# Corners of gathered taps summed by identity products on TensorE, with corner weights in PSUM

## The chip, the cores and the metric

One NeuronCore of a Trainium2 chip runs the kernel. The metric is the device time of one execution in microseconds (us).

## The reference

A feature map x of 256 channels and 32 x 32 pixels, float32, goes through four blocks. Block 0 is a masked bottleneck of grouped convolutions with a residual. Blocks 1 and 2 are bottlenecks around a **deformable 3 x 3 convolution** of 64 channels: a small convolution gives for each pixel and each of nine taps a displacement, block 1 also a factor (a sigmoid), the 64 channels are sampled at the displaced place by bilinear interpolation, and the samples are contracted with the 3 x 3 weights. Block 1 has group norms, block 2 has biases. Block 3 is a non-local block (theta, phi, g) with a normalisation over pixels. Of the sampling, per tap:

```python
out = g(y0, x0) * (wy0 * wx0)[:, None, :] + g(y0, x0 + 1) * (wy0 * wx1)[:, None, :] + g(y0 + 1, x0) * (wy1 * wx0)[:, None, :] + g(y0 + 1, x0 + 1) * (wy1 * wx1)[:, None, :]
```

where g looks up 64 channels at an integer pixel, and gives zero outside the image.

## The kernel before

The program is written by hand, one instruction stream per engine, with semaphores between them. The blocks follow one another. All the change lies in the sampling of blocks 1 and 2, which the code calls b = 0 and b = 1 and this text the first and the second **sampling loop**.

The nine taps are computed in two ways at once. Three of them, the **dense** taps, need no gather: for each of 8 tiles of 128 source pixels ScalarE writes |y distance| into PSUM (L751, "near"), VectorE turns it into a hat function times the x hat (L558, "product", output S, one of four buffers which show in the profile as S, x and mask), and TensorE multiplies with the 64 channels (L937, "dense"): 3 x 8 = 24 **chunks** per loop, each of two matmuls, one for each half of the 1024 pixels. For each of these taps TensorE first spreads x position, y position and, in the first loop, the modulation over 128 partitions (L923, "positions": one matmul per half of the pixels), and ScalarE reads these two halves out (L709, L731, L721). The two halves go to two PSUM banks, `B_FILL = [1, 3]`, which later taps use again.

The other six taps are **gathered**. GpSimd issues 48 indirect DMAs per loop (L348: 8 tiles of 128 pixels x 6 taps), each of which fetches for 128 pixels all four corners x 64 channels into G. G holds five tiles. The work on them goes in 16 **units** u per loop, two for each tile: 4 taps (even u), then 2 taps (odd u). For one unit VectorE multiplies the four corners with their weights (L571, GW, weights from the SBUF tile corner_w), adds them pairwise (L579, GA) and once more (L586, GS). TensorE transposes GS, two taps at a time (L981: 2 transposes or 1), ScalarE copies the result to SBUF (L778, sT), and TensorE contracts it with the weights two units later (L951).

The order is written out. On VectorE unit u is GW, one product, GA, further products, GS. The table BESIDE says how many chunks stand beside each unit: `[0, 0, 2, 1, 3, 2, 2, 2, 2, 2, 2, 2, 2, 1, 1, 0]`. On TensorE unit u is its chunks, the contraction of unit u - 2, a wait for GS of u and for the copy sT of u - 1, the transposes, in units 0 and 1 some matmuls that keep the clock up (L823, 6 and 2 of them), and the positions of a later tap where one is due. In the last two units of the second loop there are two residual matmuls each (L835), and after unit 15 come two of `last_conv3` (L893). On ScalarE unit u is its near chunks, the copy sT, and the reading of positions.

## Time and profile before

| | |
|---|---|
| median of 3 runs | 242.93 us (242.92 to 243.75) |
| profiled execution: span from the first to the last instruction | 242.3 us |
| mean granted TensorE clock | 0.872 |
| PE, DVE, ACT, POOL busy | 191.5, 169.3, 110.8, 116.2 us |
| first loop: first gather to last gather issued | 37.4 to 107.4 us |
| second loop: first gather to last gather issued | 140.7 to 209.5 us |

Only the span is given for the profiled execution; the median of the runs lies 0.6 us above it. PE is TensorE's matmuls, PEld its weight loads, DVE VectorE, ACT ScalarE, POOL GpSimd, SP the queue that issues plain DMAs. Times on the axis are from the first instruction. A float32 matmul shows as two records in the trace, so that "x4" in a row of L937 is the two matmuls of one chunk; a transpose or an fp32r matmul shows as one. A row of several records gives the time from the start of the first to the end of the last, and each matmul's duration holds its way through the array besides the time for which it occupies it.

### The profile page before, as it was taken

How to read it: one execution, taken by the hardware profiler on the slowest of the kernel's cores; microseconds unless marked ns; L12 is line 12 of the kernel's file. 1: busy time of each engine (PE TensorE's matmuls, PEld its weight loads, DVE VectorE, ACT ScalarE, POOL GpSimd, SP SyncE). 2: the span in 40 equal slices, each digit the busy share in tenths (PEclk: the TensorE clock that was granted, in tenths of full speed). 3: DMA queues.
4: the chain of work that ended last, by engine and by line, in shares of the span. 5: the costliest groups of instructions: out<-in, count | busy, mean ns of one | idle time of the engine just before them, and what ended most of it. 6: DMA issues, size and time to landing. Idle time of an engine off the chain costs nothing. (4 is left out here: it accounts for less than half of the span.)

```text
span 242.3 us, 2580 instructions
## 1 busy us (share of the span) xinstructions
PE 191.5 (79%) x894; PEld 106.8 (44%) x894; DVE 169.3 (70%) x276; ACT 110.8 (46%) x163; POOL 116.2 (48%) x111
## 2 busy tenths in 40 slices
PE   8997998767678959749977989395796868799920
PEld 8362957553222423316763677352332323334500
DVE  1996624698999999964375343989999799522362
ACT  2122303567969866301106133769798562034022
POOL 5000006777787787750010067787788777400010
PEclk9999998559997997995999975589999979999855
DMA  6500022323322222230000223323322233300004
GB/s 228 225 0 3 0 87 65 105 72 98 97 88 88 89 65 87 87 108 1 3 0 0 87 62 99 102 80 98 104 68 66 87 97 99 87 3 0 0 0 173
DMA packets 7887, 17.60 MB, mean 73 GB/s; under 512 B 1729, under 2 KB 3906, under 8 KB 7746
## 3 DMA queue, kind: packets, MB, share of 16 engines
q0 software_dynamic: 4608, 12.59, 17.2%
q1 hardware_dynamic: 3122, 4.32, 5.1%
q10 hardware_dynamic: 144, 0.52, 0.5%
q8 instruction: 7, 0.11, 0.2%
q14 instruction: 6, 0.05, 0.1%
HBM read 15.33 MB, written 2.10 MB: 72 GB/s over the span
## 5 line engine op out<-in xcount | busy, mean ns | idle before, releaser
L348 POOL DMA_INDIRECT G<-table,idx x96 | 110.1, 1147 | 53.8 <-issue 43.2
L751 ACT ACTIVATE ps<-pos_y,second 128x1024 f32<-128x1024 f32 x48 | 52.9, 1115 | 17.6 <-DVE S L558 8.5
L981 PE MATMUL ps<-first,GS 128*128 128x128 f32 x48 | 13.3, 334 | 31.7 <-DVE GS L586 31.6
L571 DVE TENSOR_TENSOR GW<-G,corner_w 128x1024 f32<-128x1024 f32 (+1 forms) x32 | 30.6, 955 | 7.1 <-DMA G<-table,idx 6.9
L335 POOL TENSOR_TENSOR rstd<-var,half_neg 128x1 f32<-128x1 f32 (+1 forms) x4 | 2.6, 639 | 63.5 <-DVE var L398 39.7
L558 DVE SCALAR_TENSOR_TENSOR x<-ps,hat_x 128x1024 f32<-128x1024 f32 x24 | 29.1, 1213 | 0.0
L823 PE MATMUL ps<-first 128*128 128x128 f32 x180 | 28.2, 314 | 0.0
L823 PEld LDWEIGHTS ps<-first 128*128 128x128 f32 x180 | 25.8, 224 | 4.2 <-issue 3.9
L937 PE MATMUL ps<-x,V 128*64 128x512 f32 x96 | 27.1, 643 | 0.0
L981 PEld LDWEIGHTS ps<-first,GS 128*128 128x128 f32 x48 | 5.8, 149 | 39.8 <-DVE GS L586 38.3
L778 ACT ACTIVATE sT<-ps 128x256 f32<-128x256 f32 (+1 forms) x32 | 10.3, 322 | 27.5 <-PE ps L981 27.5
L951 PEld LDWEIGHTS ps<-sT,second 128*64 128x64 f32 x96 | 12.6, 147 | 19.4 <-issue 17.3
L579 DVE TENSOR_TENSOR GA<-GW 128x512 f32<-128x512 f32 (+1 forms) x32 | 17.5, 547 | 0.2
L951 PE MATMUL ps<-sT,second 128*64 128x128 f32 x96 | 16.9, 291 | 0.4 <-ACT sT L778 0.4
L558 DVE SCALAR_TENSOR_TENSOR mask<-ps,hat_x 128x1024 f32<-128x1024 f32 x12 | 14.6, 1215 | 1.9 <-ACT ps L751 1.9
L558 DVE SCALAR_TENSOR_TENSOR S<-ps,hat_x 128x1024 f32<-128x1024 f32 x12 | 14.6, 1216 | 0.1
L937 PE MATMUL ps<-S,V 128*64 128x512 f32 x48 | 14.3, 676 | 0.0
L923 PE MATMUL ps<-om_split,sel 128*128 128x512 f32 x30 | 12.9, 529 | 1.5 <-DVE VS L490 1.5
L937 PE MATMUL ps<-mask,V 128*64 128x512 f32 x48 | 13.4, 640 | 0.0
L586 DVE TENSOR_TENSOR GS<-GA 128x256 f32<-128x256 f32 (+1 forms) x32 | 11.2, 349 | 0.4
L709 ACT ACTIVATE near_x<-ps,second 128x512 f32<-128x512 f32 x12 | 7.6, 683 | 7.6 <-PE ps L923 7.6
L937 PEld LDWEIGHTS ps<-x,V 128*64 128x64 f32 x96 | 6.2, 144 | 10.6 <-issue 9.9
(135 smaller groups left out, 254.6 us busy)
## 6 DMA issues: line engine op xcount, KB each, us to landing
G<-table,idx POOLq DMA_INDIRECT x96, 2.8
second<-in_second SPq DMA_DIRECT2D x1, 1432.5 KB, 8.5
table<-feat_t SPq DMA_DIRECT2D x4, 256.0 KB, 2.2
out<-x SPq DMA_DIRECT2D x4, 256.0 KB, 2.2
x<-in_x ACTq DMA_DIRECT2D x1, 512.0 KB, 4.7
x<-in_x SPq DMA_DIRECT2D x1, 512.0 KB, 5.5
first<-in_first SPq DMA_DIRECT2D x1, 224.0 KB, 4.5
at_w<-in_w_b SPq DMA_DIRECT2D x1, 1.0 KB
```

The source lines that it names most:

```text
L348: pool.indirect_dma_start(out=G[:, done % RING, k, :], out_offset=None, in_=table[b], in_offset=bass.IndirectOffsetOnAxis(ap=idx[b][:, n:n ...
L558: dve.scalar_tensor_tensor(out=S[cd % SRING], in0=near(cd), scalar=1.0, in1=hat_x[:, c // TILES], op0=ALU.min, op1=ALU.mult).then_inc(s_S, 1)
L571: dve.tensor_tensor(GW[:, :, k0:k1].rearrange("p c k e -> p k c e"), G[:, (b * TILES + t) % RING, k0:k1].rearrange("p k (c e) -> p k c e", ...
L579: dve.tensor_tensor(GA[:, :, k0:k1], GW[:, 0:2, k0:k1], GW[:, 2:4, k0:k1], ALU.add).then_inc(s_ga, 1)
L586: dve.tensor_tensor(GS[:, t % 2, k0:k1], GA[:, 0, k0:k1], GA[:, 1, k0:k1], ALU.add).then_inc(s_gs, 1)
L751: act.activation(near(cd), pos_y[:, (b * DENSE + i) % 2], ACT.Abs, bias=fld["own"][:, 1 + t:2 + t]).then_inc(s_ny, 1)
L778: act.activation(sT[:, t % 2, q.start:q.stop], ps[:, B_ST, q.start * P:q.stop * P] .rearrange("p (q n) -> p q n", n=P), ACT.Copy).then_inc ...
L823: pe.matmul(ps[:, bank, 0:P], operand, operand, start=True, stop=True)
L923: mm = pe.matmul(dst, sel[:, i, axis, :], half(om_split, h), start=True, stop=True)
L937: mm = pe.matmul(ps[side(h), B_C1, :], V2[:, t, :] if i == 2 else V[:, t, i, :], half(S[(b * CHUNKS + c) % SRING], h), start=False, stop=( ...
L951: mm = pe.matmul(ps[side(t // 4), B_C1, t % 4 * P:(t % 4 + 1) * P], w[:, q, :], sT[:, t % 2, q], start=False, stop=(u == UNITS - 1 and q = ...
L981: mm = pe.transpose(ps[:, B_ST, q * P:(q + 1) * P], GS[:, t % 2, 2 * q:2 * q + 2, :].rearrange("p k e -> p (k e)"), ident)
```

## The change

In four steps:

- VectorE still multiplies the corners with their weights (GW), but GA and GS are gone with their two tiles and two semaphores. GW becomes double (by tile), and the multiplication waits for TensorE's work on unit u - 4.
- TensorE sums instead. In place of each transpose stand four matmuls that accumulate in the same PSUM place, GW of one corner as the stationary operand and the identity as the moving one.
- The corner weights move from SBUF to PSUM bank 3.
- Bank 3 is then no longer free for positions. Both halves use bank 1: TensorE fills half 0, waits until ScalarE has read it, and fills half 1.

```diff
--- before.py
+++ after.py
@@ -79,7 +79,8 @@
 B_TPG = [1, 0]
 B_OM = 2
 B_ST = 2
-B_FILL = [1, 3]
+B_FILL = 1
+B_CW = 3
 B_NEAR = 4
 B_SMALL = 3
 B_OFF = 4
@@ -142,13 +143,10 @@
         absd = sb("absd", [P, 2, 2, NP])
         hat = sb("hat", [P, 2, 2, NP])
         sig = sb("sig", [P, NP])
-        corner_w = sb("corner_w", [P, NP * CORNERS])
         hat_m = sb("hat_m", [P, 2, NP])
         idx = [sb(f"idx{b}", [P, NP], I32) for b in range(2)]
         G = sb("G", [P, RING, GTAPS, PATCH])
-        GW = sb("GW", [P, CORNERS, GTAPS, HID])
-        GA = sb("GA", [P, 2, GTAPS, HID])
-        GS = sb("GS", [P, 2, GTAPS, HID])
+        GW = sb("GW", [P, 2, CORNERS, GTAPS, HID])
 
         sel = sb("sel", [P, DENSE, 3, P], F32R)
         V = sb("V", [P, TILES, 2, HID])
@@ -181,6 +179,7 @@
         mt = sb("mt", [D, D])
         at_w = sb("at_w", [D + 1, C])
         ps = ctx.enter_context(nc.psum_tensor("ps", [P, 8, 512], F32))
+        corner_w = ps[:, B_CW, 0:NP * CORNERS]
         table = [nc.dram_tensor(f"table{b}", (N // 2, 2, P), F32, kind="Internal").ap()
                  for b in range(2)]
 
@@ -221,8 +220,6 @@
         s_gather = [[[sem(f"s_gather{b}_{t}_{part}") for part in range(len(PARTS))]
                      for t in range(TILES)] for b in range(2)]
         s_gw = sem("s_gw")
-        s_ga = sem("s_ga")
-        s_gs = sem("s_gs")
         s_sel = sem("s_sel")
         s_omhi, s_omlo = sem("s_omhi"), sem("s_omlo")
         s_V = sem("s_V")
@@ -285,7 +282,7 @@
             return fills.index((b, PREPARE[i][axis], axis, i))
 
         def fill_bank(b, i, axis, h):
-            return B_FIRST[axis] + h if i == 0 and axis < 2 else B_FILL[h]
+            return B_FIRST[axis] + h if i == 0 and axis < 2 else B_FILL
 
         def fill_before(b, i, axis):
             n = fill(b, i, axis)
@@ -529,7 +526,7 @@
                     then(dve.tensor_tensor(hat_m[:], hat[:, :, 1, :],
                                            sig[:, None, :].to_broadcast([P, 2, NP]), ALU.mult))
                     hy = hat_m[:]
-                w4 = corner_w[:].rearrange("p (n x y) -> p n x y", x=2, y=2)
+                w4 = corner_w.rearrange("p (n x y) -> p n x y", x=2, y=2)
                 hx = hat[:, :, 0, :]
                 dve.tensor_tensor(
                     w4, hx.rearrange("p r n -> p n r")[:, :, :, None].to_broadcast([P, NP, 2, 2]),
@@ -566,25 +563,15 @@
                     done = b * UNITS + u
                     w = corner_w[:, (t * GTAPS + k0) * CORNERS:(t * GTAPS + k1) * CORNERS]
                     dve.wait_ge(s_gather[b][t][part], 16 * (k1 - k0))
-                    if done >= 2:
-                        dve.wait_ge(s_gs, done - 1)
+                    if done >= 2 * len(PARTS):
+                        dve.wait_ge(s_st, done - 2 * len(PARTS) + 1)
                     dve.tensor_tensor(
-                        GW[:, :, k0:k1].rearrange("p c k e -> p k c e"),
+                        GW[:, t % 2, :, k0:k1].rearrange("p c k e -> p k c e"),
                         G[:, (b * TILES + t) % RING, k0:k1].rearrange("p k (c e) -> p k c e", e=HID),
                         w.rearrange("p (k c) -> p k c", c=CORNERS)[:, :, :, None]
                         .to_broadcast([P, k1 - k0, CORNERS, HID]), ALU.mult).then_inc(s_gw, 1)
-                    if chunks:
-                        product(chunks.pop(0))
-                    dve.wait_ge(s_gw, done + 1)
-                    dve.tensor_tensor(GA[:, :, k0:k1], GW[:, 0:2, k0:k1], GW[:, 2:4, k0:k1],
-                                      ALU.add).then_inc(s_ga, 1)
                     for c in chunks:
                         product(c)
-                    dve.wait_ge(s_ga, done + 1)
-                    if done >= 4:
-                        dve.wait_ge(s_st, done - 3)
-                    dve.tensor_tensor(GS[:, t % 2, k0:k1], GA[:, 0, k0:k1], GA[:, 1, k0:k1],
-                                      ALU.add).then_inc(s_gs, 1)
 
 
             dve.wait_ge(s_c1[1], 1)
@@ -913,12 +900,13 @@
                         for h in range(2):
                             if i == 0 and axis == 1 and h:
                                 pe.wait_ge(s_weigh, 4 * b + 2)
-                            if fill_bank(b, i, axis, h) == B_FILL[h] and u < BESIDE.index(2):
-                                pe.wait_ge(s_weigh, 4 * b + 4)
-                                pe.wait_ge(s_dist, 2 * b + 2)
-                                pe.wait_ge(s_sig, 2)
-                            if fill_before(b, i, axis):
-                                pe.wait_ge(s_free[h], fill_before(b, i, axis))
+                            if fill_bank(b, i, axis, h) == B_FILL:
+                                if u < BESIDE.index(2):
+                                    pe.wait_ge(s_weigh, 4 * b + 4)
+                                if h:
+                                    pe.wait_ge(s_free[0], fill(b, i, axis) + 1)
+                                elif fill_before(b, i, axis):
+                                    pe.wait_ge(s_free[1], fill_before(b, i, axis))
                             dst = ps[:, fill_bank(b, i, axis, h), :]
                             mm = pe.matmul(dst, sel[:, i, axis, :], half(om_split, h),
                                            start=True, stop=True)
@@ -974,12 +962,14 @@
                     if u == UNITS - 1:
                         for late in range(u - LAG + 1, u):
                             contract(late)
-                    pe.wait_ge(s_gs, done + 1)
+                    pe.wait_ge(s_gw, done + 1)
                     if done >= 1:
                         pe.wait_ge(s_sT, done)
                     for q in pairs(u):
-                        mm = pe.transpose(ps[:, B_ST, q * P:(q + 1) * P],
-                                          GS[:, t % 2, 2 * q:2 * q + 2, :].rearrange("p k e -> p (k e)"), ident)
+                        for c in range(CORNERS):
+                            mm = pe.matmul(ps[:, B_ST, q * P:(q + 1) * P],
+                                           GW[:, t % 2, c, 2 * q:2 * q + 2, :].rearrange("p k e -> p (k e)"),
+                                           ident, start=(c == 0), stop=(c == CORNERS - 1))
                     mm.then_inc(s_st, 1)
                     if sum(BESIDE[:u + 1]) == 0:
                         keep_clock(0, IDLE[8 + u])
```

VectorE's stream in units 4 to 6 of the first loop (S, x and mask are the four buffers of the product). Before:

```order
L571 TENSOR_TENSOR GW<-G,corner_w 128x4x4x64
L558 SCALAR_TENSOR_TENSOR x<-ps,hat_x 128x1024
L579 TENSOR_TENSOR GA<-GW 128x2x256
L558 SCALAR_TENSOR_TENSOR mask<-ps,hat_x 128x1024
L586 TENSOR_TENSOR GS<-GA 128x256
L571 TENSOR_TENSOR GW<-G,corner_w 128x2x4x64
L544 TENSOR_TENSOR hat_x<-hat_x,m 128x1024
L558 SCALAR_TENSOR_TENSOR S<-ps,hat_x 128x1024
L579 TENSOR_TENSOR GA<-GW 128x2x128
```

And with the change:

```order
L568 TENSOR_TENSOR GW<-G,ps 128x4x4x64
L555 SCALAR_TENSOR_TENSOR x<-ps,hat_x 128x1024
L555 SCALAR_TENSOR_TENSOR mask<-ps,hat_x 128x1024
L568 TENSOR_TENSOR GW<-G,ps 128x2x4x64
L541 TENSOR_TENSOR hat_x<-hat_x,m 128x1024
L555 SCALAR_TENSOR_TENSOR S<-ps,hat_x 128x1024
```

The two additions of each unit have left the stream, and the multiplication reads its weights from ps, the PSUM.

TensorE's stream at units 1 and 2 of the first loop (L981 the transposes, L951 the contractions, L923 the positions; `s_free0` and `s_free1` say that ScalarE has read half 0 and half 1). Before:

```order
L981 MATMUL ps<-first,GS 128x128 [waits s_sT,s_gs]
L823 MATMUL ps<-first 128x128 x2
L923 MATMUL ps<-om_split,sel 128x512 [waits s_sig,s_free0,s_dist,s_weigh]
L923 MATMUL ps<-om_split,sel 128x512 [waits s_sig,s_free1,s_dist,s_weigh]
L934 MATMUL ps<-hat_x,VS 64x512 [waits s_weigh,s_S]
```

And with the change:

```order
L970 MATMUL ps<-first,GW 128x128 [waits s_sT,s_gw]
L970 MATMUL ps<-first,GW 128x128 x3
L810 MATMUL ps<-first 128x128 x2
L911 MATMUL ps<-om_split,sel 128x512 [waits s_free1,s_weigh]
L911 MATMUL ps<-om_split,sel 128x512 [waits s_free0,s_weigh]
L922 MATMUL ps<-hat_x,VS 64x512 [waits s_weigh,s_S]
```

One transpose has become four matmuls. The second positions matmul, which waited for an earlier tap's half 1, waits for half 0 of its own tap, and the dense chunks stand behind it.

## Rows read from the trace of the kernel before

**Rows 1.** Page of the profile: TensorE's matmuls and its granted clock in 40 slices.
```profile
PE   8997998767678959749977989395796868799920
PEclk9999998559997997995999975589999979999855
```

**Rows 2.** Chain of waits that ended last: start us, us, what.
```profile
140.74 1.02 POOL G L348
...
208.58 0.95 POOL G L348
209.53 23.81 issue
```

**Rows 3.** Page, costliest groups: busy us, mean ns, idle before and its releaser.
```profile
L348 POOL DMA_INDIRECT G<-table,idx x96 | 110.1, 1147 | 53.8 <-issue 43.2
...
L981 PE MATMUL ps<-first,GS 128*128 128x128 f32 x48 | 13.3, 334 | 31.7 <-DVE GS L586 31.6
...
L579 DVE TENSOR_TENSOR GA<-GW 128x512 f32<-128x512 f32 (+1 forms) x32 | 17.5, 547 | 0.2
...
L586 DVE TENSOR_TENSOR GS<-GA 128x256 f32<-128x256 f32 (+1 forms) x32 | 11.2, 349 | 0.4
```

**Rows 4.** Timeline of POOL: start us, us, engine, operation, idle before and releaser.
```profile
37.36 1.16 POOL L348 DMA_INDIRECT G<-table,idx  x1 [10.62 <-DVE idx L510]
...
106.42 0.95 POOL L348 DMA_INDIRECT G<-table,idx  x1 [0.30 <-issue]
...
158.97 1.72 POOL L348 DMA_INDIRECT G<-table,idx  x1 [0.30 <-issue]
...
169.04 0.95 POOL L348 DMA_INDIRECT G<-table,idx  x1 [0.30 <-issue]
```

**Rows 5.** Timeline of DVE, second loop.
```profile
152.87 1.22 DVE L571 TENSOR_TENSOR GW<-G,corner_w 128x1024 f32<-128x1024 f32 x1
...
158.66 1.21 DVE L571 TENSOR_TENSOR GW<-G,corner_w 128x1024 f32<-128x1024 f32 x1
...
168.97 1.21 DVE L558 SCALAR_TENSOR_TENSOR x<-ps,hat_x 128x1024 f32<-128x1024 f32 x1
...
208.79 1.23 DVE L571 TENSOR_TENSOR GW<-G,corner_w 128x1024 f32<-128x1024 f32 x1 [2.25 <-DMA G<-table,idx]
```

**Rows 6.** Timeline of PE, second loop.
```profile
155.33 0.69 PE L981 MATMUL ps<-first,GS 128*128 128x128 f32 x2 [4.18 <-DVE GS L586]
...
161.36 1.03 PE L937 MATMUL ps<-S,V 128*64 128x512 f32 x4
162.22 1.03 PE L937 MATMUL ps<-x,V 128*64 128x512 f32 x4
163.08 0.60 PE L951 MATMUL ps<-sT,second 128*64 128x128 f32 x4
...
167.94 0.33 PE L981 MATMUL ps<-first,GS 128*128 128x128 f32 x1 [2.67 <-DVE GS L586]
168.02 0.71 PE L923 MATMUL ps<-om_split,sel 128*128 128x512 f32 x2
...
211.53 1.88 PE L835 MATMUL ps<-x,first 128*128 128x512 f32 x4
...
214.40 1.98 PE L893 MATMUL ps<-hid,second 64*128 64x512 f32 x4
216.31 0.32 PE L951 MATMUL ps<-sT,second 128*64 128x128 f32 x1
```

**Rows 7.** Timeline of PE between the loops, matmuls of 128x128 back to back.
```profile
116.03 2.92 PE L823 MATMUL ps<-first 128*128 128x128 f32 x24
```

**Rows 8.** Windows: us, PE busy, PEld, DVE, ACT, POOL, PEclk, DMA share, GB/s.
```profile
50.00:60.00 10.00, 7.05 (x35) 4.79 (x36) 9.75 (x14) 6.74 (x10) 7.87 (x8) 0.80 0.25 79
...
153.00:158.00 5.00, 2.67 (x13) 2.67 (x14) 4.93 (x7) 3.64 (x5) 3.78 (x5) 0.50 0.26 80
158.00:163.00 5.00, 4.79 (x22) 2.49 (x22) 4.63 (x7) 3.00 (x6) 4.09 (x4) 0.81 0.26 79
```

**Rows 9.** Timeline of ACT, second loop.
```profile
166.18 0.36 ACT L778 ACTIVATE sT<-ps 128x256 f32<-128x256 f32 x1
...
176.69 1.26 ACT L709 ACTIVATE near_x<-ps,second 128x512 f32<-128x512 f32 x2
```

**Rows 10.** Timeline of PE, start and end of the first loop.
```profile
51.30 0.69 PE L981 MATMUL ps<-first,GS 128*128 128x128 f32 x2 [1.78 <-DVE GS L586]
...
112.05 0.69 PE L951 MATMUL ps<-sT,second 128*64 128x128 f32 x2 [0.37 <-ACT sT L778]
```

## The prediction

> **What bounds the kernel now.** I read the chain of waits first. From 140.7 to 209.5 us it is GpSimd issuing gathers, and their gaps of 0.30 us are issue, not waits: GpSimd waits for nobody in the second loop [rows 2]. 48 gathers of 1147 ns are the largest group of POOL, and twice that number runs in all [rows 3]. The timeline of POOL shows that a gather takes 0.95 us alone, 1.25 us with its gap, and that some take far longer [rows 4]. The long ones stand under one kind of VectorE work: the gather at 158.97 took 1.72 us, and it began 0.31 us into a GW multiplication whose two inputs lie in SBUF; the one at 169.04 took 0.95 us, and it began just as near to the start of a product that reads PSUM and SBUF [rows 4, 5]. With no such stretching the 47 steps of 1.25 us would need 58.8 us, where the first loop takes 106.42 - 37.36 = 69.1 us and the second 208.58 - 140.74 = 67.8 us [rows 2, 4]. VectorE is nearly full in the middle of the loop, and only for its last units does it wait for a gather, 2.25 us at 208.79 [rows 5]. TensorE is the engine with room: its transposes waited 31.7 us for GS in all [rows 3], in both loops together.
>
> So before the change gathers and VectorE share the bound, and TensorE has some 15 us of slack in each loop. The question is whether the work that moves to it fits there.
>
> **VectorE's part.** The additions GA and GS go, 17.5 + 11.2 = 28.7 us, 14.3 us per loop [rows 3]. What is left per loop is GW, 8 x (1.13 + 0.61), and 24 products of 1.13 us from start to start, 41 us in the first reading of both; that is not a bound. The multiplication with its weights in PSUM I cost as before (1.21 us), since the product that reads PSUM takes 1.21 us too [rows 5].
>
> **The gathers' part.** GW then has one input in SBUF, like the product, and the stretching should go: 69.1 - 58.8 = 10.3 us in the first loop (less some 2 us, as the multiplication L544 keeps two SBUF inputs) and 9.0 us in the second. This is what the change would bring if TensorE kept pace. The Trainium skill (SBUF — State Buffer, Who interferes with whom) has the rule behind it: a VectorE instruction with two SBUF inputs contends with a GpSimd instruction that reads SBUF, and one with a single SBUF input does not. The trace agrees with it at both gathers named.
>
> **TensorE's part.** Each of the 24 pairs of taps in a loop had one transpose, a single record. It gets four float32 matmuls of 128x128, two records each, so 8 records. The trace has matmuls of this very shape and type back to back at full clock: 24 records in 2.92 us, less 0.275 us for the last one's way through the array, over 23 steps: 0.115 us a record [rows 7]. A pair costs 8 x 0.115 = 0.92 us, a loop 24 x 0.92 = 22.1 us. That exceeds the slack, so I add up all that TensorE must do in one loop, as if it never waited for data (its fill bank apart). The second loop:
>
> - corner sums 22.1 us
> - 24 dense chunks, 0.86 us from start to start [rows 6]: 20.6 us; the three VS pairs ahead of each dense tap have the same form, 2.7 us with their hand-over
> - 24 contractions of 2 x 0.11 us (four records in 0.60 us less 0.27 us, over three steps [rows 6]): 5.3 us
> - 16 clock-keeping records: 1.8 us; 8 positions matmuls (two take 0.71 us, their way through included [rows 6]; I take 0.21 us each): 1.7 us
> - 4 residual matmuls, 1.88 us for two [rows 6]: 3.7 us; the last convolution before the last contraction, from 214.40 to 216.31 us [rows 6]: 1.9 us
> - half clock at the start: the granted clock is 0.50 up to 158 us and 0.81 in the next window [rows 8], so full from about 159.5 us, 4.2 us after TensorE's first transposes. If it again takes 4.2 us of work, half of that is lost: 2.1 us
> - waits at the fill bank, priced next: 4.6 us
>
> The sum is 66.5 us. It starts when GW of unit 0 is ready, 152.87 + 1.22 = 154.1 us [rows 5], and ends at **220.6 us**, where the last contraction now starts at 216.3 us [rows 6]: **+4.3 us**.
>
> The first loop, from 50.1 us (1.2 us before its first transpose at 51.30 [rows 10], as GA and GS fall away): 22.1 + 20.6 + 2.7 + 5.3 + 1.8, 12 positions matmuls 2.5, half clock 2.0 (window 50 to 60 at 0.80 [rows 8]), six fill waits 6.9, makes 63.9 us, so 114.0 us, and 0.5 us more for the last copy sT, which nothing hides there: 114.5 us against 112.05 us [rows 10]: **+2.5 us**.
>
> **The fill bank.** For a tap whose positions go to bank 1, TensorE fills half 0 and stands until ScalarE has read it. ScalarE first makes the copy sT of the unit, 0.36 us, then reads half 0, about 0.63 us [rows 9], and hand-overs and the matmul's way add some 0.15 us more than the fill itself: 1.15 us a wait. Behind it stand dense chunks that are ready, so it is all on TensorE's path. There are six such waits in the first loop after unit 0 (taps 2 and 3, three axes) and four in the second. The modulation of the first tap is filled before unit 0, while VectorE still multiplies; I cost it at nothing. Never shown alone in the trace, such a wait costs at least 0 us if TensorE would have waited for data anyway, and at most the 1.15 us and a near of 1.1 us ahead of it on ScalarE; I take 1.15 us, as ScalarE gets idler.
>
> After the loops nothing changes but the moment at which they end. Sum: 242.3 + 4.3 + 2.5 = 249.1 us of span; the median lay 0.6 us above the span, so **249.7 us**.
>
> **Rule against row.** By the rows a record of 128 columns occupies TensorE for 0.115 us [rows 7]. The Trainium skill (TensorE: Matmul & The Clock Gate, Back-to-back issue gap) gives about 81 ns for a matmul of 128 columns in a stream with its weight loads. By this a pair would cost 0.65 us and a loop 6.5 us less, and both loops together would end at some 237 us. The row is for the float32 form that this kernel has, so I follow the row and keep the other as a rival.
>
> **Rivals.**
> - *TensorE keeps pace roughly* (other side). The price of its sum is overstated by the clock or the fill waits: without the fill waits (11.5 us) and with half of the early half clock, the sum gives 249.7 - 11.5 - 2 = 236 us, with half of the fill waits hidden 243 us. For it: TensorE idles 2.67 us before 167.94 while ScalarE and VectorE work [rows 6], so some wait may fall where it would idle anyway. Against it: in the sum it never idles otherwise. The point that decides: TensorE's list per loop must be shorter by 6.8 us in both loops together. Range 236 to 244 us, chance 0.12, half of it faster by over 0.5%.
> - *Gathers set the end in both loops*: 242.9 - 8.3 - 9.0 = 226 us. This needs a corner record at under half of 0.115 us, which a transpose's single record suggests and the row of the same form denies. Chance 0.03.
> - *A corner record is cheaper than the row of its form says.* A transpose handles the same 128 columns in one record, so a pair of taps lies between one record per corner (4 x 0.115 = 0.46 us) and two (0.92 us). At the middle, 0.69 us, a loop is 5.5 us shorter, which gives 239 us. Chance 0.03. The gap that the Trainium skill (TensorE: Matmul & The Clock Gate, Back-to-back issue gap) states would make it 237 us, as above.
> - *The clock falls in the new waits.* In the middle of the loops the clock fell after idle times of some 2 us, as the slices at 7 and 5 show [rows 1]. If the waits at the fill bank or a late S bring it down, each fall costs about 1.7 us (a chunk takes twice its 0.86 us); three to six falls make 255 to 260 us. Chance 0.07.
> - *The stretching of the gathers stays*, because it hangs on the kind of instruction and not on where the weights lie. Then the last gather is issued near 207 us instead of 199.5 us, and lands 1.8 us later; TensorE's list still has more than its last unit to do by then. The time would be the same, so this is no case of its own.
>
> **The numbers.** The forecast (TensorE is the bound, 243 to 255 us) has 0.75, of which 0.04 lies within 0.5% of before; 0.5%, 1.2 us, is about what a measurement of this kernel can tell from no change. With the rivals: faster 0.06 + 0.03 + 0.03 = 0.12, within 0.5% 0.04 + 0.06 = 0.10, slower 0.71 + 0.07 = 0.78. The range: below, fill waits at half price and a corner record at 0.110 us give 243 us; above, every fill wait at 1.7 us (+5.5 us) give 255 us. It leaves out 0.12 below and 0.07 above.
>
> **What would show it.** In the changed profile TensorE should have hardly any idle time between unit 2 and the end of each loop except some 1.1 us before the second positions matmul of a tap, and VectorE should idle, waiting for TensorE (dense, through the S buffers) rather than for gathers. The gathers should take 0.95 us nearly all, so that the last one of the second loop is issued some 59 us after the first. The corner records should start 0.11 to 0.12 us apart. The last contraction should start near 114.5 us and near 223 us (220.6 us plus the first loop's 2.5 us). The forecast is wrong if the corner records come closer together than 0.10 us, if the idle time of TensorE adds up to more than 8 us beside the fill waits, or if the loops end within 2 us of the last gather's landing.

## The result, and the profile after

The changed kernel takes **257.0 us** (median of 4 runs, 255.28 to 258.76) against 242.93 us (4 runs, 242.73 to 243.75): a ratio of 1.060, with a 95% interval of 1.055 to 1.066. The forecast was 249.7 us in a range of 243 to 255 us. The direction and the engine that sets the end were right. The sum of that engine's work was too small, and the time lies above the range.

The execution that was profiled took 255.37 us, with a span of 252.8 us; the four spans are 252.8, 252.7, 256.8 and 255.9 us. (Of the runs further down, 375.05 us of c_after and 262.32 us of b_psumw are two disturbed ones, with mean clocks of 0.552 and 0.691; the ratios in the tables compare undisturbed runs alone.) The page, in its first sections: busy time by engine, then TensorE's matmuls and its granted clock in 40 slices (as [rows 1]), then the costliest groups (as [rows 3]).

```profile
span 252.8 us, 3153 instructions
...
PE 221.6 (88%) x1230; PEld 142.8 (56%) x1230; DVE 145.2 (57%) x212; ACT 111.7 (44%) x163; POOL 98.2 (39%) x111
...
PE   8989989699798899999959995988988999999930
...
PEclk9999995589999999999999975699999999999955
...
L345 POOL DMA_INDIRECT G<-table,idx x96 | 92.1, 960 | 53.8 <-issue 43.2
L970 PE MATMUL ps<-first,GW 128*128 128x128 f32 x384 | 54.0, 293 | 3.0 <-DVE GW L568 3.0
...
L568 DVE TENSOR_TENSOR GW<-G,ps 128x1024 f32<-128x1024 f32 (+1 forms) x32 | 29.9, 944 | 0.1
...
L911 PE MATMUL ps<-om_split,sel 128*128 128x512 f32 x30 | 15.8, 566 | 10.4 <-ACT near_x L696 3.6
```

VectorE lost 24 us of work and TensorE gained 30. A gather takes 960 ns in the mean where it took 1147 [rows 3]: the stretching is gone. TensorE waited 31.7 us for GS before [rows 3]; for GW it waits 3.0 us in all, and in one place, ahead of unit 0 of the second loop. Of the 10.4 us before the positions matmuls (L911), 8.9 us are the waits at the single fill bank; the other 1.5 us, a wait for VectorE's VS ahead of the first loop, were there before the change.

**Where the time came from.** Start of the first gather (F), issue of the last (G) and start of the last contraction (C) of each loop, in both timelines:

| us | span | F1 | G1 | C1 | F2 | G2 | C2 | F1 to C1 | C1 to F2 | F2 to C2 | C2 to end |
|---|---|---|---|---|---|---|---|---|---|---|---|
| before | 242.3 | 37.36 | 106.42 | 112.05 | 140.74 | 208.58 | 216.31 | 74.7 | 28.7 | 75.6 | 26.0 |
| changed | 252.8 | 36.71 | 96.69 | 117.84 | 144.95 | 203.83 | 227.75 | 81.1 | 27.1 | 82.8 | 25.0 |

The gathers finish 9.7 us and 4.8 us earlier, and nobody needs them then. The contraction that followed the last gather by 5.6 and 7.7 us now follows it by 21 and 24 us. The loops cost 6.4 and 7.2 us more; the stretch between them gives 1.6 us back, the tail 0.9, the start 0.7: 10.5 us in all.

The timeline of TensorE in the second loop, from unit 0 to unit 3, then unit 14 and the last contraction (start, us, engine, line, operation, idle before and releaser; as [rows 6]), and below it the end of the first loop (as [rows 10]):

```profile
157.13 3.78 PE L970 MATMUL ps<-first,GW 128*128 128x128 f32 x16 [3.00 <-DVE GW L568]
160.71 2.12 PE L810 MATMUL ps<-first 128*128 128x128 f32 x12
162.67 1.06 PE L970 MATMUL ps<-first,GW 128*128 128x128 f32 x8
163.56 0.61 PE L810 MATMUL ps<-first 128*128 128x128 f32 x4
...
168.38 0.60 PE L939 MATMUL ps<-sT,second 128*64 128x128 f32 x4
168.91 2.05 PE L970 MATMUL ps<-first,GW 128*128 128x128 f32 x16
170.90 1.08 PE L925 MATMUL ps<-x,V 128*64 128x512 f32 x4
171.80 0.38 PE L939 MATMUL ps<-sT,second 128*64 128x128 f32 x2
172.12 1.16 PE L970 MATMUL ps<-first,GW 128*128 128x128 f32 x8
173.03 0.47 PE L911 MATMUL ps<-om_split,sel 128*128 128x512 f32 x1
174.26 0.50 PE L911 MATMUL ps<-om_split,sel 128*128 128x512 f32 x1 [0.76 <-ACT pos_y L718]
...
220.25 2.05 PE L970 MATMUL ps<-first,GW 128*128 128x128 f32 x16
222.14 1.88 PE L822 MATMUL ps<-x,first 128*128 128x512 f32 x4
...
227.75 0.32 PE L939 MATMUL ps<-sT,second 128*64 128x128 f32 x1
```

```profile
117.84 0.43 PE L939 MATMUL ps<-sT,second 128*64 128x128 f32 x2 [0.37 <-ACT sT L765]
```

A full unit has 16 corner records and a half unit 8. After 166 us the only rows with a bracket are those of the second half of a fill. The windows say the same from there to the end of the loop (us, PE busy, PEld, DVE, ACT, POOL, clock, DMA share, GB/s; as [rows 8]):

```profile
166.00:186.00 20.00, 18.38 (x108) 10.38 (x106) 14.00 (x13) 15.30 (x20) 15.12 (x17) 1.00 0.34 106
186.00:206.00 20.00, 19.25 (x119) 11.43 (x116) 14.99 (x14) 13.38 (x17) 14.21 (x16) 1.00 0.35 106
206.00:227.50 21.50, 21.50 (x120) 12.87 (x118) 6.63 (x8) 4.56 (x9) 0.00 (x0) 1.00 0.01 1
```

TensorE is full at full clock, VectorE is at 14 to 15 of 20 us, and in the last 21.5 us no gather runs at all. VectorE waits for TensorE now, by way of ScalarE's near chunks. Its timeline in the second loop:

```profile
159.86 1.21 DVE L568 TENSOR_TENSOR GW<-G,ps 128x1024 f32<-128x1024 f32 x1
...
168.74 1.23 DVE L555 SCALAR_TENSOR_TENSOR mask<-ps,hat_x 128x1024 f32<-128x1024 f32 x1 [4.54 <-ACT ps L738]
```

One view misleads. The chain of waits still runs over the gathers of the second loop, and then has one piece of "issue":

```profile
203.83 0.95 POOL G L345
204.78 39.09 issue
```

Before, that piece was 23.8 us long [rows 2]. An engine that never waits leaves nothing for the chain to follow back, so the chain jumps over its work and lands on the last thing that was waited for. A long "issue" after the last row of an engine can mean that the bound lies elsewhere; here the windows show that it does, and where.

### The profile page after: what moved, and what is told of

It is laid out like the page before. It is cut to its first block and busy times, and to the rows that moved or that the text cites. A ratio compares the mean times of both kernels' runs of the same rounds, so it can differ in the third digit from the quotient of the medians.

```text
span 252.8 us, 3153 instructions
## 1 busy us (share of the span) xinstructions
PE 221.6 (88%) x1230; PEld 142.8 (56%) x1230; DVE 145.2 (57%) x212; ACT 111.7 (44%) x163; POOL 98.2 (39%) x111
## 5 line engine op out<-in xcount | busy, mean ns | idle before, releaser
L345 POOL DMA_INDIRECT G<-table,idx x96 | 92.1, 960 | 53.8 <-issue 43.2
L970 PE MATMUL ps<-first,GW 128*128 128x128 f32 x384 | 54.0, 293 | 3.0 <-DVE GW L568 3.0
L970 PEld LDWEIGHTS ps<-first,GW 128*128 128x128 f32 x384 | 48.2, 202 | 8.3 <-issue 4.3
L765 ACT ACTIVATE sT<-ps 128x256 f32<-128x256 f32 (+1 forms) x32 | 10.5, 328 | 49.8 <-PE ps L970 49.8
L568 DVE TENSOR_TENSOR GW<-G,ps 128x1024 f32<-128x1024 f32 (+1 forms) x32 | 29.9, 944 | 0.1
L925 PE MATMUL ps<-x,V 128*64 128x512 f32 x96 | 25.3, 605 | 0.0
L911 PE MATMUL ps<-om_split,sel 128*128 128x512 f32 x30 | 15.8, 566 | 10.4 <-ACT near_x L696 3.6
L810 PE MATMUL ps<-first 128*128 128x128 f32 x180 | 24.7, 287 | 0.0
L810 PEld LDWEIGHTS ps<-first 128*128 128x128 f32 x180 | 22.1, 197 | 4.0 <-issue 3.8
L911 PEld LDWEIGHTS ps<-om_split,sel 128*128 128x128 f32 x30 | 6.6, 228 | 16.0 <-ACT pos_y L718 4.4
L925 PE MATMUL ps<-S,V 128*64 128x512 f32 x48 | 12.5, 601 | 0.0
```

Of the source, the lines that this page charges most:

```text
L345: pool.indirect_dma_start(out=G[:, done % RING, k, :], out_offset=None, in_=table[b], in_offset=bass.IndirectOffsetOnAxis(ap=idx[b][:, n:n ...
L568: dve.tensor_tensor(GW[:, t % 2, :, k0:k1].rearrange("p c k e -> p k c e"), G[:, (b * TILES + t) % RING, k0:k1].rearrange("p k (c e) -> p ...
L765: act.activation(sT[:, t % 2, q.start:q.stop], ps[:, B_ST, q.start * P:q.stop * P] .rearrange("p (q n) -> p q n", n=P), ACT.Copy).then_inc ...
L810: pe.matmul(ps[:, bank, 0:P], operand, operand, start=True, stop=True)
L911: mm = pe.matmul(dst, sel[:, i, axis, :], half(om_split, h), start=True, stop=True)
L925: mm = pe.matmul(ps[side(h), B_C1, :], V2[:, t, :] if i == 2 else V[:, t, i, :], half(S[(b * CHUNKS + c) % SRING], h), start=False, stop=( ...
```

## The experiments

The theory (T): each loop is as long as TensorE's list of work, which is the corner sums, the dense chunks and the waits at the fill bank; gathers and VectorE no longer matter. Rival A: VectorE or the gathers hold the end. Rival B, for the waits at the fill bank: they are only the place where a wait shows, and it would appear elsewhere if it were taken away there. Each kernel has 4 runs, unless a run count is given; kernels of one set ran on one chip, with the kernel before beside them. In the tables "loops" are the two distances from the first gather to the last contraction, in the profiled execution.

### First set: the weights, the banks, the price of a record

The changed kernel again, and three edits of it. e_sbufw puts the corner weights back into SBUF. e_sbufw_2banks gives each half of the positions its own bank again besides. e_fp32r has TensorE read GW and the identity as fp32r, the form for which this kernel splits its positions into a high and a low part (om_split); no run measures what it does to the values of GW.

```diff
# e_sbufw
-        corner_w = ps[:, B_CW, 0:NP * CORNERS]
+        corner_w = sb("corner_w", [P, NP * CORNERS])
# e_sbufw_2banks, besides
-B_FILL = 1
+B_FILL = [1, 3]
...
-                                if h:
-                                    pe.wait_ge(s_free[0], fill(b, i, axis) + 1)
-                                elif fill_before(b, i, axis):
-                                    pe.wait_ge(s_free[1], fill_before(b, i, axis))
...
+                            if fill_before(b, i, axis):
+                                pe.wait_ge(s_free[h], fill_before(b, i, axis))
# e_fp32r
-        GW = sb("GW", [P, 2, CORNERS, GTAPS, HID])
+        GW = sb("GW", [P, 2, CORNERS, GTAPS, HID], F32R)
+        ident_r = sb("ident_r", [P, P], F32R)
...
-                                           ident, start=(c == 0), stop=(c == CORNERS - 1))
+                                           ident_r[:], start=(c == 0), stop=(c == CORNERS - 1))
```

> The changed kernel again, as the control on this chip. Theory T (TensorE's list of work is the bound in both loops): 255 to 259 us, span about 252.8 us, last contractions 81 us (first loop) and 83 us (second loop) after the first gather. A rival that puts the loss on a clock that fell by chance in the first profile expects clearly less than 255 us here.

> Only the place of the corner weights is undone (SBUF again); the single fill bank and the sums on TensorE stay. Theory T: within 1.5 us of the changed kernel, since TensorE is the bound and has 15 us or more of work left when the last gather lands; the gathers stretch again (mean about 1050 ns or more against 960 ns). Rival A (gathers still set the end, or reading the weights from PSUM is what costs VectorE time): 5 us or more away from the changed kernel, slower by the first and faster by the second.

> Corner weights in SBUF and two fill banks again; only the sums on TensorE are left of the change. Theory T: the ten waits between the halves of a positions pair (6.5 us in the first loop, 4.4 us in the second by the profile of the changed kernel) and 0.8 us before unit 0 go, so 10 to 12 us less than with the single bank: about 245 us. Rival B (these waits fall where TensorE would idle anyway): less than 3 us gained.

> The changed kernel with GW and the identity in fp32r, so that a corner sum matmul is one record at one column a cycle, the numbers being rounded by that form. Theory T: a pair costs 4 x 0.055 = 0.22 us in place of 0.89 us, 16 us less for TensorE in each loop; the loops are then bound by the gathers (last one about 59.5 us after the first, 4 us to land, multiply and sum) and by VectorE, so 225 to 233 us, under the kernel before. Rival C (VectorE, ScalarE or the chain between them is the bound, and TensorE only looks full): within 4 us of the changed kernel.

| kernel | median (range), us | span | loops, us |
|---|---|---|---|
| before (7 runs) | 243.57 (238.77 to 244.8) | | |
| c_after | 258.39 (257.57 to 375.05) | 255.8 | 81.1, 84.4 |
| e_sbufw | 256.26 (254.52 to 257.96) | 252.7 | 81.1, 82.8 |
| e_sbufw_2banks | 246.03 (243.44 to 246.48) | 244.4 | 76.2, 80.1 |
| e_fp32r | 242.07 (240.01 to 243.03) | 241.0 | 74.6, 76.2 |

**The weights.** With them in SBUF the gathers are stretched again: the last of the first loop is issued 66.8 us after the first, where it was 60.0 us in the changed kernel. The loops are the same to 0.03 us. So the one thing that the change gained, the shorter gathers, is worth nothing as long as TensorE sets the end. T holds, and A falls for the changed kernel.

**The bank.** Two fill banks give 10 us back by the median (256.26 to 246.03) and 8 by the profiled spans, most of the loss. In both kernels TensorE's list is the bound; the group of positions matmuls in the page of e_sbufw_2banks has 1.5 us of idle time before it where the changed kernel had 10.4:

```profile
L910 PE MATMUL ps<-om_split,sel 128*128 128x512 f32 x30 | 12.8, 528 | 1.5 <-DVE VS L487 1.5
```

With the second bank kept, the corner sums cost 1.5 us in the first loop and 4.5 in the second, 6.0 together. The single bank costs 4.9 and 2.7 us on top (81.1 to 76.2 and 82.8 to 80.1), so it is the dearer part of the change. The second loop's 2.7 us for the bank are too few, and its 4.5 us for the sums too many: the corner sums of e_sbufw_2banks start 14.0 us after the first gather there and those of e_sbufw 12.2 us, and executions of one kernel differ by as much (12.2 us in the changed kernel, 14.2 us in c_after). From the first corner sum to the last contraction the single bank costs 4.7 us in the first loop (67.5 against 62.8) and 4.5 us in the second (70.6 against 66.1).

**The record.** An fp32r matmul shows as one record, and I expected half the length for it as well. The timeline of e_fp32r has, for one full unit (four corners, two pairs):

```profile
61.08 1.11 PE L972 MATMUL ps<-ident_r,GW 128*128 128x128 f32 x8
62.03 0.44 PE L913 MATMUL ps<-om_split,sel 128*128 128x512 f32 x1
64.13 0.50 PE L913 MATMUL ps<-om_split,sel 128*128 128x512 f32 x1 [1.66 <-ACT m L710]
```

8 records take 0.95 us: 0.16 us from the first to the second, 0.112 us from each to the next behind it, where I had expected 0.055. Half the records at the same length shorten a loop by 11 us and not by 16. The loops show 6.5 us of it in the first and 6.6 to 8.2 in the second: in the first units TensorE now waits longer for ScalarE, as the 1.66 us at a fill in the last row, and once in each loop the granted clock falls: it is 0.50 from 69.0 to 72.4 us and from 168.0 to 171.4 us, so half of 3.4 us is lost each time. The 225 to 233 us that I expected were missed for all three reasons.

### Second set: who is next

e_hybrid lets VectorE do the first addition (GA), and TensorE sums two records of it for each pair instead of four; e_hybrid_2banks is the same with the weights in SBUF and two banks, e_fp32r_2banks the same with fp32r sums. e_noidle takes away the clock-keeping matmuls of units 0 and 1.

```diff
# e_hybrid
+                    dve.tensor_tensor(GA[:, t % 2, :, k0:k1], GW[:, 0:2, k0:k1], GW[:, 2:4, k0:k1],
+                                      ALU.add).then_inc(s_ga, 1)
...
-                        for c in range(CORNERS):
+                        for c in range(2):
# e_noidle
-IDLE = [13, 6, 14, 8, 12, 8, 10, 2, 6, 2, 4, 2, 3, 3, 1, 1]
+IDLE = [13, 6, 14, 8, 12, 8, 10, 2, 0, 0, 4, 2, 3, 3, 1, 1]
```

> The first addition on VectorE, two-matmul sums on TensorE, but weights in PSUM and the single fill bank as in the change. Theory T: as with fp32r sums, the same count of records (0.107 to 0.112 us each), so within 2 us of that run, 240 to 243 us; 4 to 8 us above the version with two banks, which is what the single bank costs.

> VectorE makes the first addition (GA) again, TensorE sums the two halves that are left (two float32 matmuls a pair); weights in SBUF, two fill banks. Theory T (TensorE's list decides until it is shorter than the gathers and VectorE's work): the list falls by 24 x 2 x 0.223 = 10.7 us a loop against the changed kernel and by the waits between halves (7.3 and 4.4 us), to some 62 to 66 us, under the end that gathers and VectorE allow, about 72 us from first gather to last contraction in place of 81 to 84 us. So 235 to 240 us, under the kernel before. Rival D (any matmul sum on TensorE costs more than the addition that it replaces): 243 us or more.

> The fp32r sums with weights in SBUF and two fill banks. In the first fp32r run a corner record took 0.107 us, not 0.055 us, and the ends came 74.6 and 76.2 us after the first gather, TensorE still without pause from unit 5 on. Theory T: the waits between halves go as well (up to 7.3 and 4.4 us), the gathers become the bound, last one issued about 64 us after the first, loops of 70 to 72 us: 232 to 237 us. Rival C (the chain through VectorE and ScalarE bounds it): 241 us or more, as with the single bank.

> The changed kernel without the 8 clock-keeping matmuls in units 0 and 1 of each loop (16 records, 1.8 us at full clock, 3 us where the clock is at half). Theory T: they stand on TensorE's path now, so each loop is 1.8 to 3 us shorter unless the clock then rises later by as much work: 251 to 254 us by this, against 255 to 258 us. Rival: no change, since the clock comes up later or ScalarE's copy sT is what unit 1 waits for.

| kernel | median (range), us | ratio to before | span | loops, us |
|---|---|---|---|---|
| before (7 runs) | 241.01 (239.34 to 244.28) | | | |
| e_hybrid | 240.63 (238.25 to 240.69) | 0.998 (0.990 to 1.006) | 238.8 | 72.8, 77.1 |
| e_hybrid_2banks | 241.11 (240.75 to 242.21) | 1.003 (0.996 to 1.010) | 239.0 | 74.9, 75.3 |
| e_fp32r_2banks | 235.17 (234.14 to 236.0) | 0.977 (0.970 to 0.984) | 233.2 | 69.4, 70.3 |
| e_noidle | 257.20 (253.68 to 260.68) | 1.055 (1.044 to 1.065) | 258.9 | 84.2, 84.2 |

**e_hybrid** came out where T had it. It has half of the corner records on TensorE and the first of the two additions on VectorE, and ends level with the kernel before, a median of 240.63 us against 241.01.

**e_hybrid_2banks** has the second bank besides and is no faster; 235 to 240 us were expected, and the 4 to 8 us between the two kernels did not show. Here the weights in SBUF count, since TensorE is no longer full and VectorE waits for gathers, as in the kernel before [rows 5]:

```profile
205.94 1.23 DVE L570 TENSOR_TENSOR GW<-G,corner_w 128x1024 f32<-128x1024 f32 x1 [2.99 <-DMA G<-table,idx]
```

**e_fp32r_2banks** beats both kernels, by 5.8 us against the one before. Its additions are off VectorE, its fills don't wait, its sums are cheap; the bound is the gathers, which its page shows with 18.9 us of VectorE's idle time:

```profile
L570 DVE TENSOR_TENSOR GW<-G,corner_w 128x1024 fp32r<-128x1024 f32 (+1 forms) x32 | 30.3, 952 | 18.9 <-DMA G<-table,idx 18.9
```

Whoever wants its time gives up the float32 form of GW, and would have to measure what that does to the result.

**e_noidle** is undecided by its time: two runs near 260.5 us, two near 253.8, and only these, on which the ratio in the table rests, lie in the 251 to 254 us of T. Its profile is of the longer pair, and shows the granted clock still at its lower level in unit 2 of the first loop, where in the changed kernel the second level is reached in unit 0. Without the extra matmuls TensorE waits 0.56 us before unit 1:

```profile
55.02 2.05 PE L970 MATMUL ps<-first,GW 128*128 128x128 f32 x8 [0.56 <-ACT sT L765]
...
59.12 1.98 PE L922 MATMUL ps<-hat_x,VS 128*64 128x512 f32 x4
```

These matmuls cost 1.8 us a loop (16 records); in two of four runs their absence cost more than it saved, in the other two it didn't. What decides between the two is not settled; there is no profile of the shorter pair.

### Third set: the wait at the fill bank taken away, and what lies between groups

If the bank's wait is TensorE's alone, it can be filled with work. e_defer puts half 1 of each fill behind the next unit's dense chunks; e_hybrid_defer is the same edit of e_hybrid. e_touch64 and e_touch128 ask another question: what it costs to go from corner sums to a matmul of another width. Each adds a one-column matmul of 64 or 128 outputs between the two pairs of a full unit, 8 in a loop; its result isn't used.

```diff
# e_defer
+                    if u:
+                        positions(u - 1, (1,))
...
-                    positions(u)
+                    positions(u, (0,))
# e_touch64 (e_touch128: 128 for 64)
                     for q in pairs(u):
+                        if part == 0 and q:
+                            pe.matmul(ps[0:64, B_ST, PAIRS * P:PAIRS * P + 1], ident[:, 0:64], ident[:, 0:1],
+                                      start=True, stop=True)
```

> The changed kernel, with the fill of half 1 put behind the dense chunks of the next unit, so that ScalarE reads half 0 while TensorE works; nothing else differs, the bank is still single. Theory T: the waits between the halves (6.5 us in the first loop, 4.4 us in the second) shrink to under 1 us in all, loops of 75 to 76 us and 78 to 80 us, in place of 81 and 83 to 84: 246 to 249 us. Rival B (ScalarE or VectorE inherits the wait, since the positions come later): under 3 us gained.

> First addition on VectorE, two-matmul sums, weights in PSUM, single bank with the deferred half. The run with two banks and weights in SBUF was held by gathers (75 us a loop, VectorE waiting for them), the one with the single bank by TensorE's waits (73 and 77 us). Theory T: with both out of the way the gathers stretch only under GA, last one 60 to 63 us after the first, loops of 69 to 72 us, 230 to 236 us, under the kernel before with exact float32 sums. Rival: 239 us or more if the sum on TensorE itself is the cost.

> The changed kernel with one more matmul (64 columns of the identity as weights, one column) between the sums of the first and the second pair of each even unit, 8 a loop: it adds two hand-overs between 128-wide and 64-wide matmuls. The trace of the changed kernel shows 0.2 us from the last corner record to a 64-wide matmul beyond its 0.11 us, and 0.1 us the other way, which the forecast left out. If hand-overs cost that, 8 x 0.3 us and the matmul's own 0.1 us: 3 us a loop more. If they cost nothing beyond the matmul itself: under 1 us a loop.

> The same additional matmul with all 128 columns of the identity as weights, so no change of width: 8 x 0.2 us at most, 0.8 to 1.6 us a loop; about 1.5 us a loop less than the one of 64 columns if the change of width is what costs, and the same if it is not.

| kernel | median (range), us | ratio to before | span | loops, us |
|---|---|---|---|---|
| before (13 runs) | 242.14 (239.27 to 243.87) | | | |
| e_defer | 258.53 (255.29 to 258.62) | 1.062 (1.051 to 1.072) | 256.6 | 80.9, 85.0 |
| e_hybrid_defer (10 runs) | 243.84 (241.93 to 244.67) | 1.011 (1.007 to 1.016) | 242.9 | 77.5, 76.3 |
| e_touch64 (1 run) | 263.67 | | 261.9 | 85.9, 87.5 |
| e_touch128 (1 run) | 258.75 | | 257.0 | 84.5, 84.6 |

**e_defer** was expected at 246 to 249 us and gained nothing. Rival B is right for this edit. TensorE no longer stands at the bank; ScalarE does, 2.38 us before 168.96 for half 1 of x, and everything that it has queued behind stands with it, among it the near chunks and the copy sT. TensorE then waits for that copy, and the clock falls right behind the wait. The timelines of ScalarE and TensorE in the second loop:

```profile
168.96 0.69 ACT L696 ACTIVATE near_x<-ps,second 128x512 f32<-128x512 f32 x1 [2.38 <-PE ps L911]
...
174.66 1.13 PE L972 MATMUL ps<-first,GW 128*128 128x128 f32 x8 [1.95 <-ACT sT L765]
...
175.95 1.98 PE L925 MATMUL ps<-mask,V 128*64 128x512 f32 x4
```

The last row is a dense chunk at twice the 1.03 us of its kind [rows 6]: the granted clock is at 1.2 GHz there, after an idle time of 1.95 us. **e_hybrid_defer** (230 to 236 us expected) failed in the same way; it waits 2.85 us for sT before 168.56 and has the clock down at 170.1. A wait can be moved off one in-order queue only if the queue that inherits it has nothing urgent behind. Whether a copy sT ahead of the second reading on ScalarE would save these two kernels wasn't tried.

**The touches** show what lies between groups. The timelines of the two kernels in the first loop, one full unit each:

```profile
94.76 1.16 PE L973 MATMUL ps<-first,GW 128*128 128x128 f32 x8
95.84 0.28 PE L970 MATMUL ps<-first 128*64 128x1 f32 x2
96.05 1.16 PE L973 MATMUL ps<-first,GW 128*128 128x128 f32 x8
97.14 1.08 PE L925 MATMUL ps<-x,V 128*64 128x512 f32 x4
```

```profile
94.05 1.16 PE L973 MATMUL ps<-first,GW 128*128 128x128 f32 x8
95.05 0.28 PE L970 MATMUL ps<-first 128*128 128x1 f32 x2
95.19 1.14 PE L973 MATMUL ps<-first,GW 128*128 128x128 f32 x8
96.26 1.08 PE L925 MATMUL ps<-x,V 128*64 128x512 f32 x4
```

8 records need 8 x 0.112 = 0.89 us. Before the 64-wide matmul 94.76 to 95.84 = 1.08 us go by, 0.19 more; before the 128-wide one 94.05 to 95.05 = 1.00 us, 0.11 more. The start times of the single records say where. In both kernels the second record of these sums, which follow 64-wide contractions, comes 0.21 us after the first, 0.10 us late; this is what the two have in common. From the last record to the added matmul it is 0.112 us where that is 128 wide, so nothing is lost, and 0.204 us where it is 64 wide, so 0.09 us is lost. Back to the sums it is 0.21 and 0.14 us with the two one-column records in it, and the second record of the sums is late again, behind the 128-wide one-column matmul too (0.19 us), so the width is not the only thing that delays it. So a unit with a 64-wide matmul between its pairs takes 2.38 us, with a 128-wide one 2.21 us, without 1.99 us. In all three the dense chunk, 64 wide, comes some 0.2 us later than the length of the records ahead of it, half of which is lost at their start and half at their end. The loops grew more than this accounts for: 4.7 us in both with e_touch64 (8 units at 0.39 us are 3.1), 3.4 and 1.8 us with e_touch128 (8 at 0.22 are 1.8). The loops' beginnings differ by 2 us between executions of one kernel (below). Counted from the first corner sum to the last contraction, the first loop takes 71.8 us in e_touch64 and 70.3 us in e_touch128, 3.2 and 1.8 us more than the 68.5 us of c_after, where the 16 records of unit 0 run at the lower clock as long; that is what the units give. Each kernel has a single run, so the rows of the unit are the measurement, and the loops bear it out.

### Fourth set: the clock at the loop's start, and the kernel before with the bank alone

Two questions were open: whether the half clock at the start of the loop costs what the forecast had, and what the PSUM weights are worth without the sums on TensorE. e_warm adds clock-keeping matmuls ahead of unit 0 (6 in the second loop, 1 in the first), where TensorE idled 3.0 us. b_psumw is the **kernel before** with two of the change's four steps, the weights in PSUM and the single fill bank; its sums stay on VectorE.

```diff
# e_warm
+                pe.wait_ge(s_dist, 2 * b + 2)
+                pe.wait_ge(s_sig, 2)
+                keep_clock(B_ST, 6 if b else 1)
                 for u in range(UNITS):
# b_psumw, against the kernel before
-B_FILL = [1, 3]
+B_FILL = 1
+B_CW = 3
...
-            corner_w = sb("corner_w", [P, NP * CORNERS])
+            corner_w = ps[:, B_CW, 0:NP * CORNERS]
```

> The changed kernel with 6 more clock-keeping matmuls in the 3.0 us for which TensorE stands before the second loop's unit 0 (and 1 in the first loop, where the gap is 0.8 us). They take time only where it stood idle. If the half clock at the start of a loop is a term of about 2 us in each loop, as the forecast had it, it falls by 1 to 2 us in the second loop, where the corner records should be at 0.11 us apart from the first or second unit on, and by less than 1 us in the first: second loop 81 to 82 us in place of 82.8 to 84.4. If the clock does not rise earlier, no change.

> The kernel before with nothing of the change but the place of the corner weights (PSUM) and with it the single fill bank with its wait; VectorE adds, TensorE transposes. Theory T: the stretching goes for GW and stays for GA and GS, TensorE's slack of some 15 us a loop takes the waits between the halves, so the loops are 1 to 3 us shorter than before (74.7 and 75.6 us), 237 to 241 us. Rival B: the waits delay VectorE and ScalarE, which are full in this kernel, and the loops get longer, over 243 us.

| kernel | median (range), us | ratio to before | span | loops, us |
|---|---|---|---|---|
| before (7 runs) | 242.87 (238.22 to 244.7) | | | |
| e_warm | 255.82 (255.16 to 256.97) | 1.068 (1.050 to 1.086) | 254.1 | 83.0, 82.8 |
| b_psumw | 243.06 (240.73 to 262.32) | 1.014 (0.983 to 1.045) | 238.9 | 75.2, 74.8 |

**e_warm.** The corner sums of unit 0 in the second loop, in e_warm and then in c_after, which begin equally long after the first gather (14.23 us):

```profile
161.30 2.31 PE L973 MATMUL ps<-first,GW 128*128 128x128 f32 x16 [0.43 <-DVE GW L568]
```

```profile
160.08 3.78 PE L970 MATMUL ps<-first,GW 128*128 128x128 f32 x16 [3.00 <-DVE GW L568]
```

1.5 us less for the same 16 records, and the loop is 1.6 us shorter (82.8 against 84.4). Most of the forecast's 2.1 us for the half clock at the start of the second loop is thereby borne out, by one profile of each kernel. In the first loop, with one matmul added, nothing was gained, where I had expected up to 1 us: its 16 records take 3.41 us as in c_after, and the 1.9 us that the loop is longer (83.0 against 81.1) lie ahead of the first corner sum, 14.4 and 12.6 us after the first gather.

**b_psumw.** The gathers' stretch shrinks from 69.1 and 67.8 us to 61.6 and 60.4, and VectorE never waits for one: before GW its page has 0.1 us of idle time.

```profile
L572 DVE TENSOR_TENSOR GW<-G,ps 128x1024 f32<-128x1024 f32 (+1 forms) x32 | 30.3, 946 | 0.1
...
L925 PE MATMUL ps<-om_split,sel 128*128 128x512 f32 x30 | 16.1, 575 | 12.3 <-ACT pos_y L732 4.7
```

Yet the loops stay at 75.2 and 74.8 us (74.7 and 75.6 before), and I had expected a gain to 237 to 241 us. From 200 to 209 us VectorE's timeline has no idle time: its list, with GA and GS still in it, sets the end. Earlier in the loops it does wait, for TensorE and for ScalarE's near chunks, 5.0 us in the first loop and 4.6 us in the second. Before, it waited 3.6 and 5.2 us, most of it for gathers. That this comes from the fill bank (10.8 of the 12.3 us in the second row) is my reading; it wasn't tried apart. The stretched gathers and VectorE's additions were two bounds at nearly the same height; taking one away shows the other. The interval of its ratio leaves open whether it is faster or slower.

## Why the prediction was short

**Right, by its steps.** *TensorE is the bound*: shown by the windows, by e_sbufw and by e_fp32r. *The stretching goes*: 960 ns against 1147 a gather, and the last gather of the second loop comes 58.9 us after the first (forecast 59). The Trainium skill's rule on two SBUF inputs (SBUF — State Buffer, Who interferes with whom), named in the forecast, agrees with the trace: e_sbufw has the one changed operand in SBUF again, and a gather takes 1053 ns in the mean against 960. *A GW multiplication that reads PSUM costs the same*: 1.21 us. *Corner records*: 0.112 us where I took 0.115, so 21.5 us a loop for 22.1; the 81 ns of the Trainium skill (TensorE: Matmul & The Clock Gate, Back-to-back issue gap) are not met by this float32 form. *The fill waits*: the halves of a fill start 1.23 to 1.43 us apart, 1.0 to 1.2 us more than a fill; six make 6.5 us (forecast 6.9) and four 4.4 us (4.6). *Half clock at the start*: in the second loop 1.8 us at unit 0 (3.58 us for 16 records of 0.112) and 0.6 us at the clock-keeping matmuls behind it (1.96 us for 12 records), 2.4 us (forecast 2.1), with e_warm behind it. In the first loop it was over-priced: 1.2 us (2.95 us for 16 records) where I had 2.0.

**The step that failed** is the sum itself: "I add up all that TensorE must do in one loop, as if it never waited for data". Each group was priced by its records back to back, and nothing was put for going from one group to the next. Measured from the first corner sum to the last contraction, the list is 117.84 - 50.35 = 67.5 us in the first loop (forecast 64.4) and 227.75 - 157.13 = 70.6 us in the second (66.5): **3.1 and 4.1 us short.** The priced terms came out near their size, so what is missing comes with the change of groups, ahead of a group or behind its first record:

- 16 corner records last 1.79 us and the dense chunk behind them starts after 170.90 - 168.91 = 1.99 us: 0.20 us, 0.10 of it between the first record and the second, 0.09 ahead of the chunk. The first part goes with coming from the 64-wide contractions, the second with going to a 64-wide matmul: ahead of the 128-wide residual matmuls it is 222.14 - 220.25 = 1.89 us, and between clock-keeping matmuls, 128 wide too, 8 records take 163.56 - 162.67 = 0.89 us, with nothing lost. In 14 units of a loop a 64-wide matmul (once last_conv3, of 64 rows, which comes as late) follows the sums, or the fill behind them (where it is as much: 174.69 less 174.26 us for a fill of 0.21 us), 2.8 us.
- the four contraction records ahead of the sums take 168.91 - 168.38 = 0.53 us for 0.44, and two 0.32 us for 0.22: some 0.09 us x 14 = 1.3 us.
- the first dense chunk behind sums or a fill takes 0.91 us and not 0.86 (170.90 to 171.80): 0.05 us in the 10 units where it wasn't priced, 0.5 us.

These make 4.6 us. The terms that came out smaller take off 0.6 us (records) and 0.2 us in the second loop or 0.4 us in the first (fill waits): 3.8 and 3.6 us. The half clock makes the difference between the loops. With its 0.3 us more the second comes to 4.1 us, which is the miss; with its 0.8 us less the first comes to 2.8 us, and some 0.3 us more stand between the six contractions of its unit 15 (115.19 to 116.31, against 223.95 to 224.75 in the second loop), which makes 3.1 us. The touches show the first item apart; the second and the third are read from rows alone. Such hand-overs stood already in the timeline that the forecast read: in the kernel before, the four contraction records that start at 163.08 [rows 6] and the transposes behind them are 0.53 us apart.

```profile
163.61 0.44 PE L981 MATMUL ps<-first,GS 128*128 128x128 f32 x2
```

I took the records' own length from those rows, not the distance to the next group; they had cost nothing as long as TensorE had slack.

**The rest of the sum**, against the forecast for both loops of 249.1 us of span:

| part | forecast, us | measured, us | difference |
|---|---|---|---|
| first gather | 37.36 | 36.71 | -0.7 |
| first gather to first corner sum, loop 1 | 12.7 | 13.6 | +0.9 |
| list, loop 1 | 64.4 | 67.5 | +3.1 |
| between the loops | 28.7 | 27.1 | -1.6 |
| first gather to first corner sum, loop 2 | 13.4 | 12.2 | -1.2 |
| list, loop 2 | 66.5 | 70.6 | +4.1 |
| tail | 26.0 | 25.0 | -0.9 |
| span | 249.1 | 252.8 | +3.7 |

The +0.9 us has two parts. The first gather started 0.7 us earlier than before, and what the first corner sum waits for didn't. Only the rest is the wait at the modulation's fill before unit 0, "I cost it at nothing", with VectorE as its cover. The cover nearly holds: the multiplication of unit 0 begins at 48.76 us and takes 1.2 us, the second half of the fill starts at 49.79, and the corner sums right behind it at 50.35, 0.25 us after the 50.1 us of the forecast. The -1.2 us of the second loop is within the 2 us by which executions of the same kernel differ there. The timeline of the first loop:

```profile
49.79 0.77 PE L911 MATMUL ps<-om_split,sel 128*128 128x512 f32 x1 [0.78 <-ACT m L708]
50.35 3.11 PE L970 MATMUL ps<-first,GW 128*128 128x128 f32 x16
53.30 1.50 PE L810 MATMUL ps<-first 128*128 128x128 f32 x12
```

The 1.6 us between the loops are a gain that I hadn't seen: in the changed kernel TensorE goes on at full clock behind the first loop, and before the change it did not. The 16 matmuls after the last contraction, before and after the change:

```profile
112.66 3.39 PE L823 MATMUL ps<-first 128*128 128x128 f32 x16
```

```profile
118.20 2.05 PE L810 MATMUL ps<-first 128*128 128x128 f32 x16
```

The same 16 records take 3.39 us in the first row and 2.05 us in the second. The stretch from C1 to F2 is 27.1 us in fourteen of the sixteen profiles, and 28.7 and 29.7 us in the two others, before and e_fp32r_2banks; in both of these the granted clock is down in the slices there. TensorE need not be full for the 27.1 us: b_psumw, with its sums on VectorE, has them too.

**The median beside the span** was the second wrong step: "the median lay 0.6 us above the span". Two kinds of number were compared. In every execution of which both are listed, the run's time lies 1.7 to 3.3 us above its own span (255.37 and 252.8 here). By this the profiled execution of the kernel before, at 242.3 us of span, took 244.0 us or more, longer than any of the four runs of the result. The last 1.6 us lie between 255.37 and the median of 257.0 us: two of the four runs have spans 3 to 4 us longer. The two profiles of this kernel show one place of it, in the second loop's beginning: the first corner sum comes 12.2 us after the first gather in one and 14.2 us in the other, though the 16 records of unit 0 take 3.6 us in both. So the 7.3 us between forecast and median are 3.7 of the span, 2.0 of span to run and 1.6 of run to median.

**The rivals.** That TensorE keeps pace (0.12) needed 6.8 us less work than the list had, and the list was 7 us longer. That the clock falls in the new waits (0.07, 255 to 260 us) gave about the right time by the wrong cause: the windows from 166 us have it at 1.00. In e_defer, e_hybrid_defer and e_fp32r the clock does fall in such waits. The case that made no difference, that stretching stays, is e_sbufw, and it made none. Two small slips of the forecast changed nothing: a clock of 0.81 from 158 to 163 us means the lower level up to 159.9 us, not 159.5, and the two terms of the lower bound give 242.0 us, not 243.

## What to carry to other kernels

When an engine with slack becomes the bound, take its list from start-to-start distances across the borders between groups, not from the length of records inside them: here 0.2 us at and behind the sums and 0.1 us ahead of them, in 14 units, were 4 us a loop, as much as the forecast loss of the second loop. Count a shared buffer that an edit takes on the way as an edit of its own: the second fill bank, given away to hold the weights, cost 8 us of span or more, and the place that the weights got by it was worth nothing. And before a wait is moved to another in-order queue, read what stands behind it there.
